# One saturating addition per half for the last sum and clip of q, and GpSimd's first product of a step behind the seeds of stage 0

## The chip, the cores and the metric

One core of one Trainium2 chip runs the whole program. The metric is the device time of that core in microseconds (us). TensorE (PE) multiplies matrices, and each of its matmuls has a weight load of its own (PEld) that overlaps the matmul before it. VectorE (DVE), ScalarE (ACT) and GpSimd (POOL) work on tiles of 128 partitions, each through its own queue in order, and the engines wait for each other by semaphores.

## The reference

The reference is a GRU over 32 steps, an attention over its states, and then a part on which this case turns: an oscillator integrated by Runge-Kutta over the same 32 steps, whose state q goes through a quantised feed-forward block at every step.

```
def _derivative(q, p, drive, coupling, bias):
    i_couple = jnp.tanh(q) @ coupling.T
    dq = q - q ** 3 / 3.0 - p + drive + i_couple + bias
    dp = EPSILON * (q + ALPHA - BETA * p)
    return (dq, dp)

def _rk4_step(q, p, drive, coupling, bias):
    dq1, dp1 = _derivative(q, p, ...)
    dq2, dp2 = _derivative(q + 0.5 * DT * dq1, p + 0.5 * DT * dp1, ...)
    dq3, dp3 = _derivative(q + 0.5 * DT * dq2, p + 0.5 * DT * dp2, ...)
    dq4, dp4 = _derivative(q + DT * dq3, p + DT * dp3, ...)
    q_next = q + DT / 6.0 * (dq1 + 2 * dq2 + 2 * dq3 + dq4)
    p_next = p + DT / 6.0 * (dp1 + 2 * dp2 + 2 * dp3 + dp4)
    q_next = jnp.clip(q_next, -CLAMP, CLAMP)
    p_next = jnp.clip(p_next, -CLAMP, CLAMP)
    return (q_next, p_next)
# per step, on q:  act_quant(q) -> silu(q @ w_gate) * (q @ w_up) -> act_quant -> @ w_down
```

q and p are 128 x 256 (256 features, batch 128), in float32; the feed-forward block has 832 middle features.

## The kernel before, in words

The GRU fills the span up to about 210 us, the attention goes to about 290 us, and the oscillator with the feed-forward block takes the rest: 32 steps of about 9.1 us. All engines follow an order written out by hand in the Python loops over t.

Features lie on partitions. q, p and all that belongs to them is held as 128 x 256: two halves m of 128 features, side by side. A step has four stages of the integration, called stage 0 to 3 here (slot 4t to 4t+3 in the code). A stage runs like this:

- DVE writes the seed (what does not go through the coupling matrix) of each half into PSUM: `seed_1` to `seed_4`, lines 1042, 1046, 1052 and 1060.
- ACT takes tanh of each half (L756) and the scaled square of both (L759). The stage's source is q itself in stage 0 and the result of the stage before in the others.
- PE adds the coupling product to the seed (`coupled`, L461), half by half, and counts s_ps for each. For half 0 it waits for the seed of half 0 and the first tanh, and then for the second tanh.
- DVE makes the cubic term (`cubic`, L1066, tile w_) from the square, and then the result of the stage (`nexts`, L1072): (PSUM times a factor) minus w_, once per half, counting s_next.

In stage 3 `nexts` puts its result into a spare part of PSUM, and a `tensor_scalar` with min and max (L1161) clips it to the new q, once per half. The new q starts the tanh of the next step, the seeds of stage 0 wait for s_next, PE transposes it (L486), and GpSimd adds it into t1.

GpSimd keeps the part that concerns p. In the order of a step: v1 (L1273, a product of p), then after both seeds of stage 0 uz and u3 (L1276, L1277, two more products of p), t1 = v1 + q (L1282), then W3 (L1290), an addition for the output (L1295), WZ (L1299), dq (L1301) and the new p (L1304). DVE carries t1 on to t2 (L1110), t3 (L1149) and t4 (L1154), from which GpSimd makes the new p.

The feed-forward block of earlier steps is woven into the same queues, one piece behind each stage. What bears on this case: on PE the seven transposes L497 behind stage 0 wait for hf, a 128 x 832 ACT operation (L775) that follows the square of stage 0; the block's second matmul pair L560 stands behind stage 3, ahead of the transposes of q; on DVE the `product` of sg and that matmul (L1085) stands right behind the seeds of stage 0, followed by the cubic term (L1066), a maximum over q (L1102), both `nexts` of stage 0 and the first seed of stage 1 (L1046). `product` waits for L560 (s_up) and for an earlier hf (s_hf).

Steps 0 to 2 differ: the feed-forward pieces come in one after another, and DVE prepares the weights in them (L983, L987).

## Time and profile before

| | us |
|---|---|
| median of 3 runs | 604.24 (603.88 to 604.67) |
| profiled execution, its own time | 603.75 |
| span of that execution | 601.70 |
| PE busy | 572.9 (95%) |
| DVE busy | 513.5 (85%) |
| ACT busy | 390.1 (65%) |
| POOL busy | 254.0 (42%) |

The profiled execution took 2.05 us beyond its span, which is what lies around the program's instructions. TensorE's mean granted clock is 0.997 of full speed. Busy time of PE includes matmuls that overlap, so 95% does not say that no other engine holds it up.

### The profile page before, as it was taken

To read this page: it belongs to the slowest core of one execution; us is meant where nothing else is said; L and a number is where in the kernel's file an instruction comes from. 1 tells how busy PE (TensorE), PEld (TensorE's weight loads), DVE (VectorE), ACT (ScalarE), POOL (GpSimd) and SP (SyncE) were. 2 spreads that over 40 slices of the span, in tenths; PEclk is the share of its full clock that TensorE was granted. 3 is DMA by queue.
4 is the path that set the end of the run, shared out by engine and by line. 5 is a ranking of instruction groups with operands and counts; after the bars stand their busy time and mean duration, and the time that the engine had idled before them with its cause. 6 is when DMAs were issued, how large, how long until landed. Compare 5 with 4: busy or idle time off the path is not lost.

```text
span 601.7 us, 15742 instructions
## 1 busy us (share of the span) xinstructions
PE 572.9 (95%) x5692; PEld 521.0 (87%) x5692; DVE 513.5 (85%) x1547; ACT 390.1 (65%) x959; POOL 254.0 (42%) x401
## 2 busy tenths in 40 slices
PE   9999999999999988999978999999999999999997
PEld 8999999999999887888867788888888888888885
DVE  3777767776777768998999999999999999999996
ACT  3554454444544453464556888898898888888885
POOL 0423323233232264240155556556555555555550
PEclk9999999999999998999999999999999999999999
DMA  8500000000000000500000000000000000000001
GB/s 259 187 2 2 1 1 2 1 1 2 1 1 1 19 3 2 190 4 3 1 1 1 11 19 16 15 19 10 18 20 10 19 20 10 19 19 11 17 19 37
DMA packets 12523, 14.97 MB, mean 25 GB/s; under 512 B 1632, under 2 KB 10144, under 8 KB 12448
## 3 DMA queue, kind: packets, MB, share of 16 engines
q1 hardware_dynamic: 12448, 13.97, 7.0%
q8 instruction: 47, 0.77, 0.5%
q14 instruction: 28, 0.23, 0.1%
HBM read 9.78 MB, written 4.19 MB: 23 GB/s over the span
## 4 chain that ended last, share of the span: by engine, by line
PE 73%; DVE 13%; ACT 11%; issue 3%; DVEq 0%; POOL 0%; ACTq 0%; POOLq 0%
PE PS L461 23%; PE PS L313 17%; PE PS L336 13%; ACT q_s L775 5%; PE PS L436 4%; PE PS L513 4%; PE PS L534 3%; PE PS L497 3%; ACT k_s L756 2%; DVE big L955 2%; PE PS L396 2%; PE PS L319 2%; DVE PS L1072 1%; ACT PS L759 1%; DVE h_s L1161 1%
## 5 line engine op out<-in xcount | busy, mean ns | idle before, releaser
L461 PE MATMUL PS<-k_s,h_s 128*128 128x128 f32 x1024 | 160.6, 284 | 4.2 <-DVE PS L1046 2.0
L461 PEld LDWEIGHTS PS<-k_s,h_s 128*128 128x128 f32 x1024 | 131.7, 191 | 21.1 <-DVE PS L1060 9.8
L313 PE MATMUL PS<-part 128*128 128x256 f32 x900 | 115.6, 286 | 0.0
L313 PEld LDWEIGHTS PS<-part 128*128 128x128 f32 x900 | 109.8, 191 | 0.0
L756 ACT ACTIVATE k_s<-h_s 128x128 f32<-128x128 f32 x256 | 69.1, 306 | 49.8 <-DVE h_s L1161 29.0
L336 PE MATMUL PS<-big,wrk 128*128 128x128 f32 x744 | 88.4, 275 | 1.7 <-DVE big L913 1.7
L336 PEld LDWEIGHTS PS<-big,wrk 128*128 128x128 f32 x744 | 85.8, 192 | 2.3 <-DVE big L913 2.3
L1229 POOL COPY h_s<-big 128x256 f32<-128x256 f32 x32 | 21.5, 671 | 128.9 <-DVE big L913 128.9
L461 PE MATMUL PS<-h_s 128*128 128x128 f32 x384 | 74.3, 275 | 0.0
L461 PEld LDWEIGHTS PS<-h_s 128*128 128x128 f32 x384 | 58.3, 192 | 0.0
L650 ACT ACTIVATE big<-big 128x256 f32<-128x256 f32 x32 | 13.3, 416 | 63.2 <-DVE big L895 63.2
L1066 DVE SCALAR_TENSOR_TENSOR h_s<-PS,h_s 128x256 f32<-128x256 f32 x128 | 52.7, 412 | 0.3 <-ACT PS L759 0.2
L1072 DVE SCALAR_TENSOR_TENSOR h_s<-PS,h_s 128x128 f32<-128x128 f32 x192 | 50.1, 285 | 2.2 <-PE PS L461 0.8
L759 ACT ACTIVATE PS<-h_s 128x256 f32<-128x256 f32 x128 | 47.2, 369 | 1.4 <-DVE part L961 1.4
L640 ACT ACTIVATE big<-PS,bg 128x256 f32<-128x256 f32 x96 | 41.2, 467 | 6.8 <-DVE bg L852 5.8
L1085 DVE SCALAR_TENSOR_TENSOR q_s<-PS,q_s 128x416 f32<-128x416 f32 x64 | 41.0, 644 | 0.8 <-PE PS L560 0.8
L652 ACT ACTIVATE big<-big 128x256 f32<-128x256 f32 x32 | 13.4, 418 | 38.9 <-DVE big L903 38.9
L1304 POOL TENSOR_SCALAR h_s<-q_s 128x256 f32<-128x256 f32 x31 | 12.5, 402 | 59.0 <-DVE q_s L1154 59.0
L1290 POOL TENSOR_TENSOR h_s<-h_s,k_s 128x256 f32<-128x256 f32 x32 | 25.0, 780 | 29.1 <-DVE q_s L1110 27.9
L899 DVE SCALAR_TENSOR_TENSOR big<-PS,bh,big 128x128 f32<-128x128 f32 x64 | 19.5, 346 | 18.0 <-ACT big L650 18.0
L1299 POOL TENSOR_TENSOR q_s<-h_s,k_s 128x256 f32<-128x256 f32 x32 | 23.9, 748 | 23.2 <-DVE PS L1052 23.2
L775 ACT ACTIVATE q_s<-q_s,mag 128x832 f32<-128x832 f32 x29 | 30.9, 1067 | 0.0
(189 smaller groups left out, 1244.9 us busy)
## 6 DMA issues: line engine op xcount, KB each, us to landing
out<-q_s SPq DMA_DIRECT2D x32, 128.0 KB, 1.7
x_s<-in_xT SPq DMA_DIRECT2D x14, 256.0 KB, 6.1
k_s<-in_wgT SPq DMA_DIRECT2D x1, 832.0 KB, 5.3
k_s<-in_wuT SPq DMA_DIRECT2D x1, 832.0 KB, 7.2
k_s<-in_wih SPq DMA_DIRECT2D x3, 256.0 KB, 4.1
wrk<-in_whh SPq DMA_DIRECT2D x3, 256.0 KB, 4.3
h_s<-in_wdT SPq DMA_DIRECT2D x1, 768.0 KB, 7.5
x_s<-in_xT SPq DMA_DIRECT2D x4, 128.0 KB, 3.6
```

Of the source, the lines that this page charges most:

```text
L313: r = pe.matmul(p, y, x, start=i == 0, stop=i == len(passes) - 1)
L336: r = pe.matmul(PS[:, bank, m * 128:(m + 1) * 128], whh_s[:, k, (m0 + m) * 128:(m0 + m + 1) * 128], hprev[:, k, :], start=k == 0, stop=k == 1)
L436: r = pe.matmul(PS[:, bank, :], raw(w), raw(x), start=k == 0 and n == 0, stop=k == 1 and n == 2)
L461: return pe.matmul(PS[:, m, 0:128], w, x, start=False, stop=True, skip_group_check=True)
L640: ac.activation(gi[:, n % 2, m, :], bulk_bank(u), ACT.Identity, bias=bg[:, m:m + 1]).then_inc(s_gi, 1)
L756: ac.activation(cm(th[slot % 2], m), cm(src, m), ACT.Tanh).then_inc(s_th, 1)
L759: ac.activation(sqP, src, ACT.Square, scale=math.sqrt(cube[s])).then_inc(s_sq, 1)
L775: ac.activation(hf[:, 0:NI], hN[i % 2], ACT.Identity, scale=h_at(i, 4), bias=mag[:, 0:1]).then_inc(s_hf, 1)
L1066: ve.scalar_tensor_tensor(w_, sqP, cube[s] * own[s], src, ALU.subtract, ALU.mult).then_inc(s_w, 1)
L1072: ve.scalar_tensor_tensor(dst(m), PS[:, m, 0:128], of_ps[slot % 4], cm(w_, m), ALU.mult, ALU.subtract).then_inc(s_next, 1)
L1085: ve.scalar_tensor_tensor(hN[i % 2][:, at], pg[:, g], q_at(i, 3), sg[:, at], ALU.mult, ALU.mult).then_inc(s_hN, 1)
L1290: po_.tensor_tensor(two(W3), two(u3), I_at(t), ALU.add).then_inc(s_W3, 1)
```

## The change

All of q's integration is now held multiplied by lam = 3/c4, with c4 = c/U as before. With that factor the last sum of stage 3 is PSUM + w_ with no factor on PSUM, and a custom DVE instruction, TENSOR_ADD_SAT, computes max(min(in0 + in1, s0), s1), which is sum and clip in one. It reads PSUM and w_, writes the new q in SBUF, and counts s_q. `nexts` of stage 3 and the two clips of L1161 are gone: four DVE instructions per step become two. Scale factors elsewhere (tanh, square, seeds, quantisation, the two start values) take up lam; they are immediates, and the copy of the start value becomes a `tensor_scalar`. The seeds of stage 0 change from `tensor_tensor` to `scalar_tensor_tensor` and wait for s_q. s_next counts six per step now (function q_next).

On GpSimd v1 waits for both seeds of stage 0 as well, and t1 comes right behind it, ahead of uz and u3.

```
+    lam = 3 / c4
+    of_ps = (3.0, 3.0, -6.0)
+    q_next = lambda t, s, m: 6 * t + 2 * s + m + 1
...
-                    ac.activation(cm(th[slot % 2], m), cm(src, m), ACT.Tanh).then_inc(s_th, 1)
+                        ac.wait_ge(s_next, q_next(slot // 4, s - 1, m))
+                    ac.activation(cm(th[slot % 2], m), cm(src, m), ACT.Tanh,
+                                  scale=(-1 if s == 3 else 1) / lam).then_inc(s_th, 1)
...
                 for m in range(2):
                     if t:
-                        ve.wait_ge(s_next, 8 * t - 1 + m)
-                    ve.tensor_tensor(PS[:, m, 0:128], I_at(t)[:, m], cm(pn[t % 2], m), ALU.subtract).then_inc(s_seed, 1)
+                        ve.wait_ge(s_q, 2 * t - 1 + m)
+                    ve.scalar_tensor_tensor(PS[:, m, 0:128], cm(pn[t % 2], m), -1 / lam, I_at(t)[:, m], ALU.mult,
+                                            ALU.add).then_inc(s_seed, 1)
...
+            def last_next(t):
+                ve.wait_ge(s_w, 4 * t + 4)
+                for m in range(2):
+                    ve.wait_ge(s_ps, 8 * t + 7 + m)
+                    ve._custom_dve(bass.dve_ops.TENSOR_ADD_SAT, out=cm(qn[(t + 1) % 2], m), in0=PS[:, m, 0:128],
+                                   in1=cm(w_, m), s0=CLAMP * lam, s1=-CLAMP * lam).then_inc(s_q, 1)
...
-                nexts(4 * t + 3, lambda m: PS[:, m, 128:256])
-                for m in range(2):
-                    ve.wait_ge(s_next, 8 * t + 7 + m)
-                    ve.tensor_scalar(cm(qn[(t + 1) % 2], m), PS[:, m, 128:256], CLAMP, -CLAMP, ALU.min,
-                                     ALU.max).then_inc(s_q, 1)
+                last_next(t)
...
+                if t:
+                    po_.wait_ge(s_seed, 8 * t + 2)
                 if t < T - 1:
                     po_.tensor_scalar(v1, p, horner[0], 0.0, ALU.mult, ALU.add).then_inc(s_v1, 1)
-                if t:
-                    po_.wait_ge(s_seed, 8 * t + 2)
-                po_.tensor_scalar(uz, p, -n3, 0.0, ALU.mult, ALU.add).then_inc(s_uz, 1)
-                po_.tensor_scalar(u3, p, -n2, 0.0, ALU.mult, ALU.add).then_inc(s_u3, 1)
-                if t < T - 1:
-                    if t:
-                        po_.wait_ge(s_q, 2 * t)
                     po_.wait_ge(s_v1, t + 1)
                     po_.tensor_tensor(t1, v1, q, ALU.add).then_inc(s_t1, 1)
+                po_.tensor_scalar(uz, p, -n3 / lam, 0.0, ALU.mult, ALU.add).then_inc(s_uz, 1)
+                po_.tensor_scalar(u3, p, -n2 / lam, 0.0, ALU.mult, ALU.add).then_inc(s_u3, 1)
```

DVE's queue before, from t4 of a step past the boundary to the first seed of the next step's stage 1; h_s and q_s are the memory in which q, the stages' results and the products lie:

```order
L1154 SCALAR_TENSOR_TENSOR q_s<-q_s,h_s 128x256
L1157 RECIPROCAL q_s<-q_s 128x1
L1072 SCALAR_TENSOR_TENSOR PS<-PS,h_s 128x128 x2
L1161 TENSOR_SCALAR h_s<-PS 128x128 x2
L1042 TENSOR_TENSOR PS<-k_s,h_s 128x128 x2
L1085 SCALAR_TENSOR_TENSOR q_s<-PS,q_s 128x416
L1066 SCALAR_TENSOR_TENSOR h_s<-PS,h_s 128x256
L1102 TENSOR_REDUCE q_s<-PS 128x1
L1072 SCALAR_TENSOR_TENSOR h_s<-PS,h_s 128x128 x2
L1046 SCALAR_TENSOR_TENSOR PS<-h_s,k_s 128x128
```

The same place now, with the new line numbers (1083 the saturating addition, 1045 the seeds of stage 0, 1096 the product, 1050 the seed of stage 1):

```order
L1165 SCALAR_TENSOR_TENSOR q_s<-q_s,h_s 128x256
L1168 RECIPROCAL q_s<-q_s 128x1
L1083 ISA h_s<-PS,h_s 128x128 x2
L1045 SCALAR_TENSOR_TENSOR PS<-h_s,k_s 128x128 x2
L1096 SCALAR_TENSOR_TENSOR q_s<-PS,q_s 128x416
L1070 SCALAR_TENSOR_TENSOR h_s<-PS,h_s 128x256
L1113 TENSOR_REDUCE q_s<-PS 128x1
L1076 SCALAR_TENSOR_TENSOR h_s<-PS,h_s 128x128 x2
L1050 SCALAR_TENSOR_TENSOR PS<-h_s,k_s 128x128
```

Only the two L1161 have left this queue; the two L1072 ahead of them have become the two L1083, and nothing else stands in another place.

GpSimd's queue before, from the new p (L1304) to W3 (L1290):

```order
L1304 TENSOR_SCALAR h_s<-q_s 128x256
L1273 TENSOR_SCALAR h_s<-h_s 128x256
L1276 TENSOR_SCALAR h_s<-h_s 128x256
L1277 TENSOR_SCALAR h_s<-h_s 128x256
L1282 TENSOR_TENSOR q_s<-h_s 128x256
L1290 TENSOR_TENSOR h_s<-h_s,k_s 128x256
```

and now (1308 the new p, 1282 v1, 1284 t1, 1285 and 1286 uz and u3, 1294 W3):

```order
L1308 TENSOR_SCALAR h_s<-q_s 128x256
L1282 TENSOR_SCALAR h_s<-h_s 128x256
L1284 TENSOR_TENSOR q_s<-h_s 128x256
L1285 TENSOR_SCALAR h_s<-h_s 128x256
L1286 TENSOR_SCALAR h_s<-h_s 128x256
L1294 TENSOR_TENSOR h_s<-h_s,k_s 128x256
```

t1, the `tensor_tensor`, has moved ahead of uz and u3, which now stand last of the four before W3.

## Rows read from the trace of the kernel before

**Rows 1.** The page's chain that ended last, shares of the span.

```profile
PE 73%; DVE 13%; ACT 11%; issue 3%; DVEq 0%; POOL 0%; ACTq 0%; POOLq 0%
```

**Rows 2.** Chain over one boundary of steps: start us, us, what.

```profile
452.08 0.20 DVE h_s L1161
...
452.31 0.51 ACT k_s L756 x2
...
453.09 1.01 ACT q_s L775
```

**Rows 3.** Timeline, same boundary: start us, us, engine, line, tiles [idle before <-releaser].

```profile
451.34 0.28 DVE L1072 SCALAR_TENSOR_TENSOR PS<-PS,h_s 128x128 f32<-128x128 f32 x1
451.44 0.40 POOL L1304 TENSOR_SCALAR h_s<-q_s 128x256 f32<-128x256 f32 x1 [1.92 <-DVE q_s L1154]
451.79 0.30 DVE L1072 SCALAR_TENSOR_TENSOR PS<-PS,h_s 128x128 f32<-128x128 f32 x1 [0.16 <-PE PS L461]
451.80 0.87 PE L560 MATMUL PS<-h_s,q_s 128*128 128x416 bf16 x4
451.93 0.41 POOL L1273 TENSOR_SCALAR h_s<-h_s 128x256 f32<-128x256 f32 x1
451.99 0.48 DVE L1161 TENSOR_SCALAR h_s<-PS 128x128 f32<-128x128 f32 x2
452.39 0.49 DVE L1042 TENSOR_TENSOR PS<-k_s,h_s 128x128 f32<-128x128 f32 x2
452.76 1.13 PE L461 MATMUL PS<-k_s,h_s 128*128 128x128 f32 x8
452.79 0.65 DVE L1085 SCALAR_TENSOR_TENSOR q_s<-PS,q_s 128x416 f32<-128x416 f32 x1
452.96 0.41 POOL L1276 TENSOR_SCALAR h_s<-h_s 128x256 f32<-128x256 f32 x1 [0.63 <-DVE PS L1042]
453.33 0.41 POOL L1277 TENSOR_SCALAR h_s<-h_s 128x256 f32<-128x256 f32 x1
453.70 0.73 POOL L1282 TENSOR_TENSOR q_s<-h_s 128x256 f32<-128x256 f32 x1
454.24 0.55 PE L497 MATMUL PS<-identh,q_s 128*128 128x128 f16 x7 [0.35 <-ACT q_s L775]
454.41 0.29 DVE L1046 SCALAR_TENSOR_TENSOR PS<-h_s,k_s 128x128 f32<-128x128 f32 x1
454.75 0.52 PEld L461 LDWEIGHTS PS<-k_s,h_s 128*128 128x128 f32 x4
```

**Rows 4.** DVE alone in a GRU step, timeline.

```profile
105.37 0.61 DVE L899 SCALAR_TENSOR_TENSOR big<-PS,bh,big 128x128 f32<-128x128 f32 x2 [0.55 <-ACT big L650]
106.01 0.42 DVE L903 TENSOR_TENSOR big<-big 128x256 f32<-128x256 f32 x1
...
107.60 0.42 DVE L909 TENSOR_TENSOR big<-big 128x256 f32<-128x256 f32 x1
108.12 0.43 DVE L913 TENSOR_TENSOR big<-big 128x256 f32<-128x256 f32 x1
```

**Rows 5.** The page's group of L899: count | busy us, mean ns | idle before.

```profile
L899 DVE SCALAR_TENSOR_TENSOR big<-PS,bh,big 128x128 f32<-128x128 f32 x64 | 19.5, 346 | 18.0 <-ACT big L650 18.0
```

**Rows 6.** Step 1, stage 0 and the start of stage 1, timeline.

```profile
307.17 0.72 POOL L1282 TENSOR_TENSOR q_s<-h_s 128x256 f32<-128x256 f32 x1
307.55 0.50 DVE L1046 SCALAR_TENSOR_TENSOR PS<-h_s,k_s 128x128 f32<-128x128 f32 x1
308.10 0.71 PE L461 MATMUL PS<-k_s,h_s 128*128 128x128 f32 x4 [1.05 <-DVE PS L1046]
```

**Rows 7.** Timeline, the product in step 2.

```profile
316.70 0.65 DVE L1085 SCALAR_TENSOR_TENSOR q_s<-PS,q_s 128x416 f32<-128x416 f32 x1 [0.80 <-PE PS L560]
```

**Rows 8.** Chain at the end of the last step.

```profile
588.32 0.70 PE PS L560 x4
589.02 0.23 PE PS L581 x2
```

More of the change, by code:

```diff
@@ L754, in stage @@
                     else:
-                        ac.wait_ge(s_next, 2 * slot - 1 + m)
-                    ac.activation(cm(th[slot % 2], m), cm(src, m), ACT.Tanh).then_inc(s_th, 1)
+                        ac.wait_ge(s_next, q_next(slot // 4, s - 1, m))
+                    ac.activation(cm(th[slot % 2], m), cm(src, m), ACT.Tanh,
+                                  scale=(-1 if s == 3 else 1) / lam).then_inc(s_th, 1)
                 if slot == 0:
                     ac.wait_ge(s_F, 16)
-                ac.activation(sqP, src, ACT.Square, scale=math.sqrt(cube[s])).then_inc(s_sq, 1)
+                ac.activation(sqP, src, ACT.Square, scale=math.sqrt(cube[s]) / lam).then_inc(s_sq, 1)
             for t in range(T):
@@ L992, in start_values @@
                 ve.wait_ge(s_S, 8)
-                ve.tensor_copy(qn[0], condf)
-                ve.tensor_scalar(pn[0], condf, SH, U, ALU.subtract, ALU.mult).then_inc(s_q0, 1)
+                ve.tensor_scalar(qn[0], condf, lam, None, ALU.mult)
+                ve.tensor_scalar(pn[0], condf, SH, U * lam, ALU.subtract, ALU.mult).then_inc(s_q0, 1)
                 ve.wait_ge(ld_cb, 16)
@@ L1050, in seed_3 @@
                 ve.wait_ge(s_W3, t + 1)
-                ve.wait_ge(s_next, 8 * t + 3 + m)
-                ve.scalar_tensor_tensor(PS[:, m, 0:128], cm(qn[t % 2], m), (1 + 2 * A * kap) / (2 * c4), cm(W3, m),
+                ve.wait_ge(s_next, q_next(t, 1, m))
+                ve.scalar_tensor_tensor(PS[:, m, 0:128], cm(qn[t % 2], m), (1 + 2 * A * kap) / 6, cm(W3, m),
                                         ALU.mult, ALU.add).then_inc(s_seed, 1)
@@ L1058, in seed_4 @@
                 for m in range(2):
-                    ve.wait_ge(s_next, 8 * t + 5 + m)
-                    ve.scalar_tensor_tensor(PS[:, m, 0:128], cm(dq, m), 1 / c4, cm(WZ, m), ALU.mult,
+                    ve.wait_ge(s_next, q_next(t, 2, m))
+                    ve.scalar_tensor_tensor(PS[:, m, 0:128], cm(dq, m), 1 / 3, cm(WZ, m), ALU.mult,
                                             ALU.add).then_inc(s_seed, 1)
@@ L1108, in vector @@
                     ve.wait_ge(s_t1, t + 1)
-                    ve.wait_ge(s_next, 8 * t + 2)
+                    ve.wait_ge(s_next, q_next(t, 0, 1))
                     ve.scalar_tensor_tensor(t2, t1, horner[1], qs[0], ALU.mult, ALU.add).then_inc(s_t2, 1)
@@ L1114, in vector @@
                         ve.wait_ge(s_wvec, 3)
-                    ve.scalar_tensor_tensor(q_at(i, 1, 3), wide(q_at(i, 0), 3), TINY, wvec[:, 0:3], ALU.max,
+                    ve.scalar_tensor_tensor(q_at(i, 1, 3), wide(q_at(i, 0), 3), TINY * lam, wvec[:, 0:3], ALU.max,
                                             ALU.mult).then_inc(s_tq, 1)
@@ L1147, in vector @@
                     ve.wait_ge(s_t2, t + 1)
-                    ve.wait_ge(s_next, 8 * t + 4)
+                    ve.wait_ge(s_next, q_next(t, 1, 1))
                     ve.scalar_tensor_tensor(t3, t2, horner[2], qs[1], ALU.mult, ALU.add).then_inc(s_t3, 1)
@@ L1152, in vector @@
                     ve.wait_ge(s_t3, t + 1)
-                    ve.wait_ge(s_next, 8 * t + 6)
-                    ve.scalar_tensor_tensor(t4, t3, horner[3], qs[2], ALU.mult, ALU.add).then_inc(s_t4, 1)
+                    ve.wait_ge(s_next, q_next(t, 2, 1))
+                    ve.scalar_tensor_tensor(t4, t3, horner[3], qs[2], ALU.mult, ALU.subtract).then_inc(s_t4, 1)
                 if t >= 2:
@@ L1181, in vector @@
             ve.wait_ge(s_red, T)
-            ve.scalar_tensor_tensor(q_at(i, 1, 3), wide(q_at(i, 0), 3), TINY, wvec[:, 0:3], ALU.max,
+            ve.scalar_tensor_tensor(q_at(i, 1, 3), wide(q_at(i, 0), 3), TINY * lam, wvec[:, 0:3], ALU.max,
                                     ALU.mult).then_inc(s_tq, 1)
@@ L1260, in gpsimd @@
                     po_.tensor_scalar(coupU, coup, U, 0.0, ALU.mult, ALU.add).then_inc(s_cp, 1)
-                    for dst, f in ((id_q1, (1 - kap) / c4), (id_s2, -kap / c4), (id_z3, (2 - 2 * kap) / c4)):
+                    for dst, f in ((id_q1, (1 - kap) / 3), (id_s2, -kap / 3), (id_z3, (2 - 2 * kap) / 3)):
                         po_.tensor_scalar(dst, ident[:, :], f, 0.0, ALU.mult, ALU.add).then_inc(s_cp, 1)
@@ L1299, in gpsimd @@
                 po_.tensor_tensor(two(WZ), two(uz), I_at(t), ALU.add).then_inc(s_WZ, 1)
-                po_.wait_ge(s_next, 8 * t + 2)
+                po_.wait_ge(s_next, q_next(t, 0, 1))
                 po_.tensor_tensor(dq, qs[0], q, ALU.subtract).then_inc(s_dq, 1)
@@ L1303, in gpsimd @@
                     po_.wait_ge(s_t4, t + 1)
-                    po_.tensor_scalar(pn[(t + 1) % 2], t4, (CLAMP - SH) * U, (-CLAMP - SH) * U, ALU.min,
+                    po_.tensor_scalar(pn[(t + 1) % 2], t4, (CLAMP - SH) * U * lam, (-CLAMP - SH) * U * lam, ALU.min,
                                       ALU.max).then_inc(s_p, 1)
```

9 lines of the change are left out of this document (4 added, 5 removed).

## The prediction

> **What bounds the kernel now.** I read the chain of waits first, then the timeline of one boundary between steps, engine by engine, because the chain names only one of the paths that meet there. The chain gives PE 73%, DVE 13% and ACT 11% of the span [rows 1]. Across a boundary it goes from the second clip (0.20 us of its own), to the two tanh, the square and the 1.01 us of L775 on ACT, and then to PE's transposes L497 [rows 2], which begin after 0.35 us of idle time [rows 3]. Read alone, this says that the clip is on the path in each step.
>
> The timeline shows a second path that is as tight. Behind the seeds of stage 0, DVE starts the product L1085 at 452.79, and from there it has no gap until L1046, the first seed of stage 1, starts at 454.41: 1.62 us of product, cubic term, maximum and two sums, back to back. L1046 ends at 454.70, and PE's weight load for stage 1 starts at 454.75 [rows 3]. That load cannot come sooner, however early L497 is done. And the product waits not only for the seeds: it reads the result of L560, whose last matmul ends at 451.80 + 0.87 = 452.67 [rows 3]. L560 is PE's work, behind stage 3, and nothing in it depends on the clip.
>
> How long after that release can the product start? From step 4 on it has two waits (s_up and s_hf). A DVE instruction with one wait starts 0.03 us after its releaser ends (L899 to L903: 105.98, 106.01); one with two starts 0.10 us after it (L909 to L913: 108.02, 108.12) [rows 4]. So the earliest start is 452.77, against 452.79 now. Up to 0.02 us of slack is all that DVE has there.
>
> **The change part by part.** *The clips, 64 instructions, and the sums, 64 that become saturating additions.* The second sum is released by PE and starts at 451.79, before and after. What follows moves up by 0.40 us on DVE: the seeds of stage 0 from 452.39 to 451.99, ending at 452.48 in place of 452.88. The second tanh starts 0.04 us after the addition ends, at 452.12 in place of 452.31 + 0.20 = 452.51, so tanh, square and L775 move by 0.39 us, and L497 could start at 453.85, before PE is done with stage 0 (452.76 + 1.13 = 453.89) [rows 2, 3]. The 0.35 us of idle time of PE goes. What is late next is the first seed of stage 1: it moves only by the product's 0.00 to 0.02 us, and PE waits for it after L497 in place of before. PE's own order ahead of the boundary is unchanged, so the gain is 0.00 to 0.02 us in each of the 29 boundaries from that into step 3 to that into step 31. I take the middle, 0.01: 29 x 0.01 = 0.3 us, with ends of 0 and 0.6.
>
> *The price of the new instruction.* No row has it. The nearest is the instruction it replaces, the same shape and operands: 0.28 to 0.30 us [rows 3]. The longest row of a 128x128 operation of DVE with a PSUM and an SBUF operand is L899, 0.346 us on average [rows 5], so I bound it at 0.28 and 0.35. A longer one would be hidden towards DVE's product and ACT by the 0.4 us just won; not towards GpSimd (below). I take 0.29, no difference. The Trainium skill (Vector Engine (DVE) Microarchitecture Reference, "Rate slope and fixed cost") says that measured programs of several micro-operations pay the same fixed cost as built-in ones; no run shown here has one, and it would give the same sum.
>
> *The seeds of stage 0* become a form that L1046 has already: 0.29 us each for one and the other [rows 3]. The scale factors are immediates of instructions that run anyway. One start-value copy changes its form, once: nothing.
>
> *GpSimd: v1 behind the seeds, t1 first.* Before, v1 ran at 451.93 to 452.34, which is just where the seeds would now stand; it would have met them. Now four instructions start behind the seeds. Seeds end at 452.48; GpSimd starts 0.08 us after its releaser (452.88, 452.96); a product takes 0.41, a dependent one starts 0.09 after the end of its source (L1304 ends at 451.84, L1273 starts at 451.93), t1 takes 0.73, and an independent one starts 0.04 before the end of the one ahead [rows 3]. That gives v1 452.56 to 452.97, t1 453.06 to 453.79, uz 453.75 to 454.16, u3 454.12 to 454.53. DVE takes t1 right behind L1046 (from 454.6), so t1 gains room; W3 waits for t2, which comes after that too, so u3 is in time. But u3 still runs when L1046 wants to start, at 454.39 to 454.41, with 0.12 to 0.14 us to go.
>
> Does that hurt? L1046 reads p and the drive, both in SBUF. In step 1 it started in the middle of t1 on GpSimd (307.17 to 307.89) and took 0.50 us in place of 0.29: it ended at 308.05, 0.16 us behind t1 [rows 6]. So it can bear a GpSimd operation that ends up to 0.29 - 0.16 = 0.13 us after its own start at no cost. u3 ends 0.12 to 0.14 after it. The cost is 0 to 0.01 us a step by these rows; I take 0. The Trainium skill (SBUF — State Buffer, "Who interferes with whom") states the rule behind this: a DVE instruction with two SBUF inputs contends with a GpSimd instruction that reads SBUF. It also says that the one that comes second "fully blocks" until the first is finished; what that would make of the time stands under the second rival.
>
> *Step 1.* There L1085 does not exist yet, and PE waits 1.05 us for L1046 [rows 6], so DVE's 0.40 us come through. The 0.21 us for which t1 held up L1046 go as well, since t1 is then nearly done, but uz and u3 now stand where t2 and the second seed want to read. I take 0.3 us of gain, with ends of 0 and 0.6. At the boundary into step 2 the product waits 0.80 us for L560 with DVE idle [rows 7]: nothing to gain. At the very end PE takes the transposes L581 right behind L560 (588.32 + 0.70 = 589.02) [rows 8]; q is there before that, so nothing either.
>
> *Sum.* 0.3 + 0.3 = 0.6 us off the profiled execution's 603.75: 603.15. The median of the runs is 604.24, 0.49 above that execution, so I forecast 604.24 - 0.6 = **603.6 us**, with 602.9 to 604.8 as this case's own range.
>
> **The rivals.** *First, the chain is right and the boundary shortens.* Then each step gains PE's idle 0.35 us before L497 [rows 3]: 29 x 0.35 = 10.2 us, 594. For it: the page's chain, and PE's large share. Against it: DVE's 1.62 us without a gap, and a product that cannot start before L560. It would take a product that gets free earlier, or a seed of stage 1 that PE does not wait for. Chance 0.12, part of the gain included.
>
> *Second, slower: the seed of stage 1 falls behind u3 on GpSimd.* The place is L1046 against u3, in the 28 steps 3 to 30. The margin is 0.13 us against 0.12 to 0.14. It decides as soon as u3 ends later than 0.13 us after the seed's start: each 0.01 us beyond that costs 28 x 0.01 = 0.28 us. A saturating addition of 0.35 us brings 0.05 to 0.06, and 28 x 0.06 = 1.7, less the 0.6 gained: 605.3. If the seed is held until u3 ends and then runs its full 0.29 us, it ends at 454.53 + 0.29 = 454.82 in place of 454.70, 28 x 0.12 = 3.4 us, less the 0.3 of step 1: 607.3. That second form is the skill's "fully blocks" read literally; the row of 0.50 us speaks against it, since full blocking would have made 0.34 + 0.29 = 0.63 [rows 6]. For the rival: the margin is thinner than what I can read. Chance 0.28.
>
> *Third, the saved DVE time is hidden and step 1 gains nothing:* 604.2, inside the forecast's own range, and not counted apart. The chance of the forecast is 0.60.
>
> **How the numbers follow.** A measurement of this kernel can tell about 0.2% from no change, 1.2 us here: 603.0 to 605.4. Of the forecast's 0.60, 0.05 falls below that. Faster: 0.12 + 0.05 = 0.17. The slower rival gives 0.25 above the limit and 0.03 below it. Same: 0.55 + 0.03 = 0.58. Slower: 0.25. The range reaches down to 602.2, which leaves out most of the first rival, and up to 607.3, the second rival's full blocking.
>
> **What would show it.** In the profile after, L497 should have no idle time behind L775, and PE's load of stage 1 should wait about 0.3 us for the seed L1050 instead; DVE should stand idle for some 0.3 us before the product L1096, released by L560. If DVE has no idle time there, the product is not bound by L560 as I say. L1050 should take 0.29 us; 0.30 or more, with u3 (L1286) ending over 0.13 us after its start, is the second rival. The saturating addition should take 0.28 to 0.30 us. The step should last 9.06 to 9.08 us; 8.7 is the first rival. The time outside of the span should stay near 2.05 us.

## The result, and the profile after

| | before | after |
|---|---|---|
| median of 20 runs each, us | 603.86 | 605.54 |
| lowest to highest | 601.86 to 604.67 | 603.47 to 606.17 |
| profiled execution, its span | 603.75, 601.70 | 605.59, 603.6 |
| median step of the oscillator (steps 3 to 30) | 9.077 | 9.125 |

The ratio of after to before is 1.0024, with a 95% interval of 1.0013 to 1.0034: slower by some 1.4 us (the two medians differ by 1.7). A step here lasts from the first seed of stage 0 to the first seed of stage 0 of the next step; its length is taken from the timeline. What lies around the span is 605.59 - 603.6 = 2.0 us, as before. Executions of every kernel, the one before included, come in two groups some 1.7 us apart (the last section shows what tells them apart), so small differences are compared within a group below.

The chain after gives ACT 3% in place of 11% and DVE 18% in place of 13%; it now lies where the prediction had put the second path:

```profile
PE 74%; DVE 18%; issue 4%; ACT 3%; DVEq 0%; POOL 0%; ACTq 0%; POOLq 0%
```

The chain of waits over the boundary that answers to [rows 2] (start us, us, what):

```profile
452.48 0.72 PE PS L562 x4
...
453.30 0.61 DVE q_s L1096
...
454.20 0.41 DVE q_s L1113
454.61 0.40 DVE h_s L1076 x2
455.01 0.26 DVE PS L1050
...
455.31 1.60 PE PS L463 x12
```

It goes from PE's matmul pair (L560 before, L562 now) through the product, the maximum, the two sums and the seed of stage 1 back to PE. The tanh, the square and the long ACT operation are off it.

The timeline of the boundary, which answers to [rows 3]:

```profile
452.30 0.29 DVE L1083 CUSTOM_DVE_ANT_0 h_s<-PS,h_s 128x128 f32<-128x128 f32 x1 [0.17 <-PE PS L463]
452.31 0.87 PE L562 MATMUL PS<-h_s,q_s 128*128 128x416 bf16 x4
452.51 0.49 DVE L1045 SCALAR_TENSOR_TENSOR PS<-h_s,k_s 128x128 f32<-128x128 f32 x2
453.15 0.41 POOL L1282 TENSOR_SCALAR h_s<-h_s 128x256 f32<-128x256 f32 x1 [0.79 <-DVE PS L1045]
453.30 0.65 DVE L1096 SCALAR_TENSOR_TENSOR q_s<-PS,q_s 128x416 f32<-128x416 f32 x1 [0.30 <-PE PS L562]
...
454.36 0.55 PE L499 MATMUL PS<-identh,q_s 128*128 128x128 f16 x7
454.71 0.41 POOL L1286 TENSOR_SCALAR h_s<-h_s 128x256 f32<-128x256 f32 x1
454.93 0.33 DVE L1050 SCALAR_TENSOR_TENSOR PS<-h_s,k_s 128x128 f32<-128x128 f32 x1
455.31 0.52 PEld L463 LDWEIGHTS PS<-k_s,h_s 128*128 128x128 f32 x4 [0.58 <-DVE PS L1050]
455.31 0.71 PE L463 MATMUL PS<-k_s,h_s 128*128 128x128 f32 x4 [0.41 <-DVE PS L1050]
```

Three things are to be seen. The transposes (L499) have no idle time in front of them any more, and PE waits 0.41 us after them for the seed L1050: the wait has changed its place. DVE stands idle for 0.30 us before the product, which starts 0.12 us after the matmul pair ends (452.31 + 0.87 = 453.18). And the seed starts at 454.93 while u3 on GpSimd (L1286) runs to 454.71 + 0.41 = 455.12; it takes 0.33 us in place of the 0.29 of [rows 3].

The two instructions over the whole run (durations in ns: shortest, median, longest):

```profile
L1050 DVE SCALAR_TENSOR_TENSOR PS<-h_s,k_s x64: 285/291/416, 298.5 to 583.9; 128x128 f32<-128x128 f32 x64
L1083 DVE CUSTOM_DVE_ANT_0 h_s<-PS,h_s x64: 270/291/293, 304.9 to 590.1; 128x128 f32<-128x128 f32 x64
```

The saturating addition costs what the sum before it cost. L1050's 64 are two kinds: the second seeds of a step have a median of 286 ns, the first ones, which meet u3, 337 ns.

Step 1, which answers to [rows 6]:

```profile
307.02 0.72 POOL L1284 TENSOR_TENSOR q_s<-h_s 128x256 f32<-128x256 f32 x1
307.64 0.29 DVE L1050 SCALAR_TENSOR_TENSOR PS<-h_s,k_s 128x128 f32<-128x128 f32 x1
...
308.02 0.68 PE L463 MATMUL PS<-k_s,h_s 128*128 128x128 f32 x4 [0.83 <-DVE PS L1050]
```

The seed takes its 0.29 us here, not 0.50; t1 ends only 0.10 us after the seed's start. Step 1 lasts 9.187 us in place of 9.866.

**The account.** The ordinary step is 0.048 us longer: 28 x 0.048 = 1.34. Single steps are longer than the ordinary one by 0.129 (step 20), 0.292 (23), 0.095 (25), 0.163 (26) and 0.258 (29), together 0.94, where before only step 22 was, by 0.161: 0.78 more. Step 1 gives back 0.68. Step 0 is 0.39 shorter, and from the first seed of step 31 to the end it takes 0.37 longer, which is the seeds' moving ahead alone. Together 1.34 + 0.78 - 0.68 - 0.39 + 0.37 = 1.4 us, which is the measured difference. (The two profiled spans differ by 1.9 us; the other 0.5 us lie ahead of the first seed.) The first part is the collision with u3; the second, over half as large, was in none of my cases.

A usual step, and step 23 at the same place, both of the kernel after, DVE alone:

```profile
457.16 0.49 DVE L1056 SCALAR_TENSOR_TENSOR PS<-h_s 128x128 f32<-128x128 f32 x2
```

```profile
512.05 0.29 DVE L1056 SCALAR_TENSOR_TENSOR PS<-h_s 128x128 f32<-128x128 f32 x1
512.59 0.30 DVE L1056 SCALAR_TENSOR_TENSOR PS<-h_s 128x128 f32<-128x128 f32 x1 [0.25 <-issue]
```

The two seeds of stage 2 follow each other without a gap in a usual step; in step 23 the second comes 0.34 us late, and its idle time has no releaser but "issue". It is the 1600th instruction recorded on DVE, where a second wait is a record of its own and counts. The others are the 1472nd (step 20), the 1729th (26) and the 1856th (29): each 64 or 65 above a multiple of 128. The one late instruction before was the 1601st. On GpSimd the 453rd is late, in step 25 (v1: idle for 1.08 us before it in place of 0.79).

### The profile page after: what moved, and what is told of

Its sections match the earlier page's. It is cut to its first block, busy times and chain, and to the rows that moved or that the text cites. A ratio compares the mean times of both kernels' runs of the same rounds, so it can differ in the third digit from the quotient of the medians.

```text
span 603.6 us, 15678 instructions
## 1 busy us (share of the span) xinstructions
PE 571.7 (95%) x5692; PEld 521.2 (86%) x5692; DVE 504.7 (84%) x1483; ACT 393.1 (65%) x959; POOL 254.8 (42%) x401
## 4 chain that ended last, share of the span: by engine, by line
PE 74%; DVE 18%; issue 4%; ACT 3%; DVEq 0%; POOL 0%; ACTq 0%; POOLq 0%
PE PS L463 22%; PE PS L315 18%; PE PS L338 13%; PE PS L562 4%; PE PS L438 4%; PE PS L515 3%; PE PS L536 3%; DVE q_s L1096 3%; DVE h_s L1076 3%; DVE big L958 2%; PE PS L398 2%; DVE q_s L1113 2%; PE PS L321 2%; DVE PS L1050 1%; PE PS L553 1%
## 5 line engine op out<-in xcount | busy, mean ns | idle before, releaser
L758 ACT ACTIVATE k_s<-h_s 128x128 f32<-128x128 f32 x256 | 71.9, 307 | 48.2 <-DVE h_s L1076 30.4
```

The costliest lines, as they stand in the source:

```text
L758: ac.activation(cm(th[slot % 2], m), cm(src, m), ACT.Tanh, scale=(-1 if s == 3 else 1) / lam).then_inc(s_th, 1)
```

## The experiments

Times are medians in us, ratios are to the kernel before beside which each kernel ran. "Full clock" is the difference to the kernel before among executions with a granted clock of 1.000 (0.999 in two) alone, "0.997" among the others; the ratio mixes both groups. A group can be small: one run for e3 at 0.997 and for e17 at full clock, two for e4 at full clock. "By steps" is the change that the steps of the one profiled execution add up to, from the first seed to the end, against the profiled execution of before.

| kernel | median (before) | ratio | step | by steps | full clock | 0.997 |
|---|---|---|---|---|---|---|
| after | 605.54 (603.86) | 1.0024 [1.0013, 1.0034] | 9.125 | +1.4 | | |
| e1 without u3 | 602.95 (603.41) | 0.9999 [0.9986, 1.0011] | 9.079 | +0.3 | 0.0 | +0.5 |
| e2 additions, old order | 603.22 (603.41) | 0.9997 [0.9985, 1.0009] | 9.079 | +0.4 | +0.2 | +0.2 |
| e3 clips, new order | 612.77 (603.41) | 1.0156 [1.0139, 1.0173] | 9.417 | +9.9 | +9.7 | +10.1 |
| e4 matmul pair first | 601.94 (603.41) | 0.9963 [0.9950, 0.9977] | 9.000 | -2.1 | -2.7 | -2.5 |
| e6 the same on before | 603.46 (602.57) | 1.0005 [0.9991, 1.0019] | 9.076 | 0.0 | 0.0 | +0.1 |
| e10 25 instructions ahead | 604.34 (602.57) | 1.0023 [1.0011, 1.0035] | 9.125 | +1.1 | +1.0 | +0.9 |
| e12 GpSimd spread | 603.11 (602.57) | 1.0006 [0.9993, 1.0018] | 9.083 | +0.3 | +0.4 | +0.1 |
| e13 spread, pair first | 597.06 (602.57) | 0.9905 [0.9889, 0.9922] | 8.863 | -5.9 | -6.1 | -6.2 |
| e16 one wait | 603.09 (602.71) | 1.0001 [0.9988, 1.0013] | 9.079 | 0.0 | -0.1 | +0.1 |
| e18 one wait, 28 ahead | 603.47 (602.71) | 0.9996 [0.9983, 1.0008] | 9.079 | -0.5 | -0.6 | -0.4 |
| e17 e13, one wait, 28 ahead | 596.90 (602.71) | 0.9894 [0.9876, 0.9911] | 8.863 | -6.8 | -7.2 | -6.7 |

The sum over the steps agrees with the timed difference within 0.6 us in each row, so an account by steps can be trusted to about that much.

### Is it u3? (e1, e2, e3)

e1 takes u3 away and makes W3 from uz, so its results of stage 2 are not those of the reference:

```
-                po_.tensor_scalar(u3, p, -n2 / lam, 0.0, ALU.mult, ALU.add).then_inc(s_u3, 1)
...
-                po_.wait_ge(s_u3, t + 1)
-                po_.tensor_tensor(two(W3), two(u3), I_at(t), ALU.add).then_inc(s_W3, 1)
+                po_.wait_ge(s_uz, t + 1)
+                po_.tensor_tensor(two(W3), two(uz), I_at(t), ALU.add).then_inc(s_W3, 1)
```

> The changed kernel with GpSimd's product u3 left out (W3 is made from uz, so the results of stage 2 differ from the reference). Theory (the first seed of stage 1, L1050, is held up by the read of u3 on GpSimd, which ends 0.19 us after the seed's start, and a step is 9.125 us long for it in place of 9.077): uz is now the last of the products and ends about 0.17 us before the seed starts, the seed takes 0.29 us in place of 0.33 and the step falls back to 9.07 to 9.08 us; about 604.2 where the changed kernel is 605.5, so 0.998 to 1.001 times the kernel before. Rival (the saturating addition itself or the wait for the second matmul pair costs the 0.05 us per step): the step stays at 9.12 us and the ratio at 1.002.

Its timeline at the seed of stage 1:

```profile
454.12 0.41 POOL L1285 TENSOR_SCALAR h_s<-h_s 128x256 f32<-128x256 f32 x1
...
454.71 0.29 DVE L1050 SCALAR_TENSOR_TENSOR PS<-h_s,k_s 128x128 f32<-128x128 f32 x1
```

GpSimd is done at 454.53 and the seed takes 0.29 us. The step falls from 9.125 to 9.079: the 0.048 us a step are u3's. The long steps 20, 23, 26 and 29 stay, with 0.126, 0.313, 0.163 and 0.259 us, so they are not u3's. Step 25 is ordinary in this run, whose GpSimd queue is shorter.

e2 keeps the saturating additions and puts GpSimd's instructions back in the order of before:

```
+                if t < T - 1:
+                    po_.tensor_scalar(v1, p, horner[0], 0.0, ALU.mult, ALU.add).then_inc(s_v1, 1)
                 if t:
                     po_.wait_ge(s_seed, 8 * t + 2)
+                po_.tensor_scalar(uz, p, -n3 / lam, 0.0, ALU.mult, ALU.add).then_inc(s_uz, 1)
+                po_.tensor_scalar(u3, p, -n2 / lam, 0.0, ALU.mult, ALU.add).then_inc(s_u3, 1)
                 if t < T - 1:
-                    po_.tensor_scalar(v1, p, horner[0], 0.0, ALU.mult, ALU.add).then_inc(s_v1, 1)
+                    if t:
+                        po_.wait_ge(s_q, 2 * t)
                     po_.wait_ge(s_v1, t + 1)
                     po_.tensor_tensor(t1, v1, q, ALU.add).then_inc(s_t1, 1)
-                po_.tensor_scalar(uz, p, -n3 / lam, 0.0, ALU.mult, ALU.add).then_inc(s_uz, 1)
-                po_.tensor_scalar(u3, p, -n2 / lam, 0.0, ALU.mult, ALU.add).then_inc(s_u3, 1)
```

> The changed kernel with GpSimd's order of the kernel before (v1 as soon as p is there, then behind the seeds of stage 0 uz, u3, t1). Theory: v1 now runs at the time at which the seeds of stage 0 want to read, so the first of them takes about 0.5 us in place of 0.29; nobody waits for that, since DVE has 0.3 us of idle time before the product and PE starts stage 0 only later. t1 ends before or with the start of the first seed of stage 1, so that seed takes 0.29 us and the step is 9.07 to 9.08 us. With what the early steps gained (about 1 us in the profile) 603.0 to 603.8, ratio 0.998 to 1.000. Rival (the collision of v1 with the seeds is what has to be kept away): the step gets longer than 9.125 us, ratio above 1.0024.

```profile
450.89 0.41 POOL L1280 TENSOR_SCALAR h_s<-h_s 128x256 f32<-128x256 f32 x1
450.95 0.69 DVE L1045 SCALAR_TENSOR_TENSOR PS<-h_s,k_s 128x128 f32<-128x128 f32 x2
...
451.75 0.65 DVE L1096 SCALAR_TENSOR_TENSOR q_s<-PS,q_s 128x416 f32<-128x416 f32 x1
```

v1 (L1280 here) now meets the seeds of stage 0: the first of them takes 0.484 us in place of 0.290 (median). It costs nothing, since DVE has 0.30 us to spare before the product: the seeds end at 451.64, the product starts at 451.75. The step is 9.079 again. So the second half of the change, moving v1 behind the seeds, avoided a collision that was free and made one that was not.

e3 does the opposite, the clips of before with GpSimd's new order:

```
-                if t < T - 1:
-                    po_.tensor_scalar(v1, p, horner[0], 0.0, ALU.mult, ALU.add).then_inc(s_v1, 1)
                 if t:
                     po_.wait_ge(s_seed, 8 * t + 2)
-                po_.tensor_scalar(uz, p, -n3, 0.0, ALU.mult, ALU.add).then_inc(s_uz, 1)
-                po_.tensor_scalar(u3, p, -n2, 0.0, ALU.mult, ALU.add).then_inc(s_u3, 1)
                 if t < T - 1:
+                    po_.tensor_scalar(v1, p, horner[0], 0.0, ALU.mult, ALU.add).then_inc(s_v1, 1)
                     if t:
...
+                po_.tensor_scalar(uz, p, -n3, 0.0, ALU.mult, ALU.add).then_inc(s_uz, 1)
+                po_.tensor_scalar(u3, p, -n2, 0.0, ALU.mult, ALU.add).then_inc(s_u3, 1)
```

> The kernel before (sum and clip apart) with GpSimd's new order alone. Theory (a seed that finds GpSimd reading ends about 0.15 us after GpSimd's operation): the seeds of stage 0 end 0.4 us later than in the changed kernel, so u3 ends 0.4 us later too, some 0.57 us after the start of the first seed of stage 1. That seed ends 0.43 us late, PE waits for it, and the step is 9.077 + 0.43 = 9.5 us in the 28 steps from 3 to 30: 12 us more, 616, ratio 1.018 to 1.021. Rival (GpSimd's order costs nothing and the saturating addition is what made the changed kernel slower): the step stays at 9.08 us, ratio 0.999 to 1.001.

```profile
458.48 0.55 POOL L1280 TENSOR_SCALAR h_s<-h_s 128x256 f32<-128x256 f32 x1
458.48 0.29 DVE L1046 SCALAR_TENSOR_TENSOR PS<-h_s,k_s 128x128 f32<-128x128 f32 x1
458.68 0.62 DVE L1110 SCALAR_TENSOR_TENSOR q_s<-q_s,h_s 128x256 f32<-128x256 f32 x1
...
459.00 0.57 POOL L1281 TENSOR_SCALAR h_s<-h_s 128x256 f32<-128x256 f32 x1
459.22 0.35 DVE L1115 SCALAR_TENSOR_TENSOR q_s<-q_s 128x3 f32<-128x3 f32 x1
...
459.49 0.29 DVE L1046 SCALAR_TENSOR_TENSOR PS<-h_s,k_s 128x128 f32<-128x128 f32 x1
...
459.83 0.52 PEld L461 LDWEIGHTS PS<-k_s,h_s 128*128 128x128 f32 x4 [0.26 <-DVE PS L1046]
```

The step grew by 0.34 us, not by the 0.43 that I had expected, and by another way. I had thought the first seed would be held by uz. It came first and uz (L1280) was held instead, 0.55 us in place of 0.41. But then t2 (L1110) was held by uz, 0.62 in place of 0.42, the three columns of L1115 by u3, 0.35 in place of 0.16, and so the second seed came late, for which PE's load waited 0.26. A collision that is not on the seed that PE waits for first can be dearer than one that is.

### How many waits (e16)

In after, v1 waits for the new p (s_p) and for both seeds (s_seed). The seeds wait for the new q, which needs the whole step, so the second wait covers the first, and v1 is behind the new p in GpSimd's own queue. e16 drops it:

```
                 if t:
-                    po_.wait_ge(s_p, t)
+                    po_.wait_ge(s_seed, 8 * t + 2)
                 else:
                     po_.wait_ge(s_q0, 1)
-                if t:
-                    po_.wait_ge(s_seed, 8 * t + 2)
```

> The changed kernel with one wait fewer ahead of v1 on GpSimd: the wait for the new p goes, since the seeds of stage 0, for which v1 waits too, have waited for it. Theory (v1 starts 0.16 us after the seeds with two waits and 0.08 us with one; so u3 ends 0.19 us after the start of the first seed of stage 1, beyond the 0.13 us that the seed can bear): v1 starts 0.08 us after the seeds, u3 ends 0.12 us after the seed's start, the seed takes 0.29 us and the step is 9.075 to 9.085 us; the long steps 20, 23, 26, 29 stay; ratio 0.999 to 1.001. Rival (the held seed has another cause than u3's end, or the second wait costs nothing): 9.125 us a step, ratio 1.0024.

```profile
450.08 0.49 DVE L1045 SCALAR_TENSOR_TENSOR PS<-h_s,k_s 128x128 f32<-128x128 f32 x2
...
450.65 0.40 POOL L1280 TENSOR_SCALAR h_s<-h_s 128x256 f32<-128x256 f32 x1 [0.72 <-DVE PS L1045]
...
452.21 0.41 POOL L1284 TENSOR_SCALAR h_s<-h_s 128x256 f32<-128x256 f32 x1
...
452.50 0.29 DVE L1050 SCALAR_TENSOR_TENSOR PS<-h_s,k_s 128x128 f32<-128x128 f32 x1
```

v1 starts 450.65 - (450.08 + 0.49) = 0.08 us after the seeds; in the kernel after it was 453.15 - (452.51 + 0.49) = 0.15. u3 ends 452.62 - 452.50 = 0.12 us after the seed's start, as the prediction had it, and the seed takes 0.288 us (median). The step is 9.079. So all but 0.002 of the 0.048 us a step comes from one wait too many ahead of v1. DVE's long steps stay (0.122, 0.291, 0.159, 0.257); step 25 is ordinary here too, where GpSimd's queue has one record fewer a step.

### Where the late instructions stand (e10, e18)

e10 puts 25 one-column memsets of a new, unused tile into DVE's queue at the start of the program; nothing else changes:

```
+        spare = sb("spare", [128, 32])
...
             ve.memset(mag[:, :], MAGIC).then_inc(s_mag, 1)
+            for j in range(25):
+                ve.memset(spare[:, j:j + 1], 0.0)
```

> The changed kernel with 25 tiny memsets (128x1, into an unused tile) at the start of DVE's queue, while DVE waits for its first loads. In the traces so far single steps are 0.1 to 0.3 us longer than the rest (steps 20, 23, 26 and 29 in the changed kernel, only step 22 in the one before), and the late DVE instruction is each time one whose number in DVE's queue is 64 more than a multiple of 128. Theory (something in DVE's queue comes late every 128 instructions; the changed kernel has 43 a step, so it falls on the seeds of stage 2 over and over, and the kernel before has 45, so it wanders): 25 more instructions ahead move it to where DVE waits for PE anyway, and the long steps go: 0.8 us less than the changed kernel, with 0.3 us less behind the last step; ratio to the kernel before 1.0005 in place of 1.0024, steps of 9.12 to 9.13 us as before. Rival (the long steps hang on the saturating addition or on chance): they stay at steps 20, 23, 26, 29, ratio 1.0024.

If the late instructions belonged to their step or their tile, they would stay. They moved: steps 20, 23, 26 and 29 are ordinary now, and steps 8 (+0.302) and 14 (+0.096) are long, where DVE's 960th and 1216th instruction stand, again 64 above a multiple of 128; steps 16 and 17 add 0.09 together. Step 25 keeps its 0.095, which is GpSimd's. Step 8, at the 960th:

```profile
369.93 0.65 DVE L1099 SCALAR_TENSOR_TENSOR q_s<-PS,q_s 128x416 f32<-128x416 f32 x1 [0.65 <-PE PS L563]
```

It is the product, 0.65 us idle in place of 0.30. The place was as I had thought, the gain was not: I had expected a ratio of 1.0005 and measured 1.0023. Only 0.34 us went, since the same number falls on other places that also count.

The traces show what else happens at these places. The page of the kernel after lists 28 transfers of instructions on one DMA queue, of 8192 bytes each (queue, kind: transfers, MB, share of 16 engines):

```profile
q14 instruction: 28, 0.23, 0.1%
```

8192 bytes are 64 for each of 128 instructions. One of these transfers starts 0.71, 0.79, 0.61 and 0.73 us after the start of the late instruction in steps 20, 23, 26 and 29, and 0.65 us after that of GpSimd's in step 25. It is so with those that cost nothing as well: over the 13 traces, 168 of the 208 DVE instructions whose number is 64 above a multiple of 128 have such a transfer starting within 1 us behind them, against 21 of 1419 at seven other places of the 128 (0, 16, 32, 48, 80, 96 and 112 above). So an instruction comes late where DVE's instructions are fetched. It doesn't wait for that transfer to arrive, since it runs before the transfer starts.

That a queue of 45 a step is not safe by itself shows in e3, which has 45: its steps 5, 14 and 22 are longer by 0.29, 0.29 and 0.24 us, 0.81 in all. Late there are GpSimd's 197th and 325th instruction, 128 apart, and DVE's 1601st, each with a transfer 0.6 to 0.8 us behind its start.

e18 is e16 with 28 memsets at the same place:

```
             ve.memset(mag[:, :], MAGIC).then_inc(s_mag, 1)
+            for j in range(28):
+                ve.memset(spare[:, j:j + 1], 0.0)
```

> The same with 28 tiny memsets at the start of DVE's queue. Theory (both losses of the changed kernel lifted: the held seed, 1.3 us, and the late instruction every 128, 0.8 us): steps of 9.08 us, at most 0.3 us in all of longer single steps between step 3 and step 30, and what step 1 gained stays; 0.5 to 0.8 us less than the kernel before, ratio 0.998 to 1.0. Rival (the place of the late instruction has nothing to do with the count): steps 20, 23, 26 and 29 are long again, 0.8 us in all, ratio 1.0 to 1.001.

Of the long steps of e16, 0.83 us together, 0.32 are left (steps 5 and 7). Against the kernel before it is 0.6 us faster at full clock and 0.4 at 0.997; e16 was level with it. The 0.5 us between them are the late instructions' share that this shift hides. The ratio over all runs, 0.9996, doesn't tell it from no change; the sum over the steps (-0.5) and both groups of runs do agree on it. This is close to what the change would have brought with neither loss. That it comes out near the 0.6 us of the prediction is luck: none of it is won at the ordinary boundaries, which were to give 0.3.

### What the freed time on DVE is worth (e4, e6, e12, e13, e17)

After the change DVE waits for the matmul pair, which stands behind other transposes. e4 puts the pair ahead of them:

```
+                if t >= 1:
+                    i = t - 1
...
+                            r = pe.matmul(pg[:, g], qiT[:, k, :], wu_q[:, k, g * 416:(g + 1) * 416],
+                                          start=k == 0, stop=k == 1)
+                    r.then_inc(s_up, 1)
                 if t >= 2:
...
                     r.then_inc(s_x1t, 1)
-                if t >= 1:
-                    i = t - 1
...
-                            r = pe.matmul(pg[:, g], qiT[:, k, :], wu_q[:, k, g * 416:(g + 1) * 416],
-                                          start=k == 0, stop=k == 1)
-                    r.then_inc(s_up, 1)
```

> The changed kernel with PE's second matmul pair of the feed-forward block ahead of the two transposes of x, so that the product's release comes 0.22 us sooner. Theory (two holds in a row: the product waits for that matmul pair, and the first seed of stage 1 waits for u3 on GpSimd): the product starts 0.2 us sooner, but the seed still ends 0.14 us behind u3 and takes 0.5 us or more; the step stays at 9.11 to 9.13 us, ratio 1.001 to 1.003. Rival (GpSimd does not hold the seed, the matmul pair alone sets the step): 8.90 us a step, 6 us less, ratio 0.992 to 0.994.

```profile
452.45 0.29 DVE L1050 SCALAR_TENSOR_TENSOR PS<-h_s,k_s 128x128 f32<-128x128 f32 x1
452.45 0.54 POOL L1286 TENSOR_SCALAR h_s<-h_s 128x256 f32<-128x256 f32 x1
452.65 0.62 DVE L1121 SCALAR_TENSOR_TENSOR q_s<-q_s,h_s 128x256 f32<-128x256 f32 x1
...
453.26 0.29 DVE L1050 SCALAR_TENSOR_TENSOR PS<-h_s,k_s 128x128 f32<-128x128 f32 x1
```

I had expected 9.11 to 9.13 us a step, all of the gain eaten by u3; it was 9.000. The seed came in just ahead of u3, which was held instead (0.54 us); the price went to t2 (L1121, 0.62 in place of 0.42) and to the second seed. The kernel is 0.37% faster than before.

e6 makes the same edit to the kernel before.

> The kernel before, with only PE's second matmul pair ahead of the two transposes of x. Theory (in the kernel before the clip keeps DVE busy up to the product, so the pair's earlier end is worth nothing without the saturating addition): the step stays at 9.07 to 9.08 us, ratio 0.999 to 1.001. Rival (the pair's place alone brings what the combination brings): 9.00 us a step or less, ratio 0.996.

Nothing, as expected: there the product's other releaser, the end of DVE's own clips and seeds, is as late as the pair. Neither edit gives much alone; the two paths are tied, and each edit shortens one.

e12 is after with GpSimd's work spread over the step: only v1, t1 and u3 right behind the seeds of stage 0, uz after W3, and the output addition behind the seeds of stage 3.

```
-                po_.tensor_scalar(uz, p, -n3 / lam, 0.0, ALU.mult, ALU.add).then_inc(s_uz, 1)
                 po_.tensor_scalar(u3, p, -n2 / lam, 0.0, ALU.mult, ALU.add).then_inc(s_u3, 1)
...
                 po_.tensor_tensor(two(W3), two(u3), I_at(t), ALU.add).then_inc(s_W3, 1)
-                if t >= 4:
-                    i = t - 4
-                    po_.wait_ge(s_x1k, i + 1)
-                    po_.wait_ge(s_osc, i + 1)
-                    po_.tensor_tensor(ob[i % 2], ob[i % 2], x1n[i % 2], ALU.add).then_inc(s_out, 1)
+                po_.tensor_scalar(uz, p, -n3 / lam, 0.0, ALU.mult, ALU.add).then_inc(s_uz, 1)
...
                 po_.tensor_tensor(dq, qs[0], q, ALU.subtract).then_inc(s_dq, 1)
+                if t >= 4:
+                    i = t - 4
+                    po_.wait_ge(s_seed, 8 * t + 8)
+                    po_.wait_ge(s_x1k, i + 1)
+                    po_.wait_ge(s_osc, i + 1)
+                    po_.tensor_tensor(ob[i % 2], ob[i % 2], x1n[i % 2], ALU.add).then_inc(s_out, 1)
```

> The changed kernel with GpSimd's work spread otherwise: behind the seeds of stage 0 v1, t1 and u3 only, uz between W3 and the seeds of stage 2, and the addition for the output behind the seeds of stage 3, where GpSimd waited 1.9 us before. Theory (the first seed of stage 1 was held by u3; with that gone the product's wait for PE's second matmul pair is what sets the step): u3 ends 0.2 us before the seed starts, the seed takes 0.29 us, a step 9.07 to 9.08 us, as in the run without u3; ratio 0.999 to 1.001. Rival (GpSimd's products merely collide elsewhere): 9.12 us or more.

Alone it takes off the collision (seed 0.293 us, step 9.083) and no more. u3 ends 0.06 us ahead of the seed's start (452.27, 452.33), not the 0.2 us that I had expected. With the pair first as well, it is e13:

> The same with PE's second matmul pair ahead of the two transposes of x. Theory (two holds, both lifted now): the product starts at the end of the seeds of stage 0, 0.35 us sooner against the boundary, the second sum of stage 0 is then released by PE, and PE starts stage 1 about 0.25 us sooner: 8.80 to 8.87 us a step, 6 to 7.5 us less than the kernel before, ratio 0.988 to 0.991. Rival (some third hold was as tight as these two, so that moving the pair brings no more than the 0.08 us it brought to the changed kernel): 9.00 us a step, ratio 0.996.

```profile
448.95 0.50 DVE L1045 SCALAR_TENSOR_TENSOR PS<-h_s,k_s 128x128 f32<-128x128 f32 x2
...
449.43 0.65 DVE L1096 SCALAR_TENSOR_TENSOR q_s<-PS,q_s 128x416 f32<-128x416 f32 x1
...
450.80 0.41 POOL L1285 TENSOR_SCALAR h_s<-h_s 128x256 f32<-128x256 f32 x1
...
451.06 0.29 DVE L1050 SCALAR_TENSOR_TENSOR PS<-h_s,k_s 128x128 f32<-128x128 f32 x1
```

The product follows the seeds at once, the seed of stage 1 starts 2.11 us after the first seed of stage 0 (in the kernel after 454.93 - 452.51 = 2.42), and u3 (L1285 here) ends 0.15 us after its start at no cost. The step is 8.863 us, the kernel 0.95% faster than before (0.9889 to 0.9922). The page's chain now names DVE first:

```profile
DVE 45%; PE 43%; issue 8%; ACT 3%; DMA 1%; SPq 1%; DVEq 0%; ACTq 0%
```

e17 adds the single wait and the 28 memsets:

> The fastest so far (GpSimd's work spread, PE's matmul pair first), with both of these edits. Theory: the seed of stage 1 does not meet u3 there, so one wait fewer brings little by itself; the long steps of 0.8 us go. A step 8.83 to 8.87 us, ratio 0.988 to 0.990 where it was 0.9905. Rival (DVE sets the step there and the late instruction costs wherever it falls, since DVE has no idle time left): the long steps move but stay 0.8 us in all, ratio 0.990 to 0.991.

It has the same step of 8.863, and 0.8 us less in the single steps. At 596.90 us (0.9894, 0.9876 to 0.9911) it is the fastest kernel of this case; against e13 it gains 0.9 us at 0.997 (597.22, 4 runs, to 598.10, 3 runs) and 1.1 at full clock, where it has one run.

## Why the prediction was wrong

The forecast was 603.6 us and no change that can be told; what came was 605.54, a loss of 0.24%. That is outside of the forecast's own 602.9 to 604.8, and inside the wide range of 602.2 to 607.3, which took in the second rival. That rival, with 0.28, was the one that happened, at its place, though not for the reason it gave, and it is 1.34 of the 2.12 us that were lost. Two steps failed: the start of GpSimd's work behind the seeds, read 0.07 us too early, and the late instructions, a cost that the sum did not have.

- *The two tied paths.* Right. PE's 0.35 us before the transposes are gone and stand, as 0.41 us, before stage 1's matmuls. The first rival, which read the chain alone, would have made the step 8.7 us.
- *The product is bound by the matmul pair.* Right: 0.30 us idle, released by L562, in each of the 29 boundaries. The gain of 0.00 to 0.02 us in each was 0: e1 and e16, with no collision, have 9.079 us against 9.077. I had taken 0.01, which is 0.3 us.
- *The price of the saturating addition.* Right: 291 ns (median), of 0.28 to 0.30 us.
- *"GpSimd starts 0.08 us after its releaser".* Wrong, and the step on which the collision hung. That 0.08 us was read before an instruction with one wait [rows 3]. v1 has two, and starts 0.15 us after. I had read in [rows 4] that a second wait costs DVE 0.07 us, and had used it for the product, but not for GpSimd, 0.07 us being just what the margin could not bear. u3 thus ends 0.19 us after the seed's start, not 0.12 to 0.14, and the seed takes 0.048 us longer: 28 x 0.048 = 1.34 us. e16 gives all but 0.06 us of it back by dropping the wait.
- *The hold itself.* The bound of 0.13 us was near: 0.12 cost nothing in e16, 0.15 next to nothing in e13 (294 ns, median), 0.19 cost 0.045. The held seed ends 0.14 us after u3, which puts the bound at 0.29 - 0.14 = 0.15, a little above mine. The Trainium skill (SBUF — State Buffer, "Who interferes with whom") says that the one that comes second is fully blocked. It says so of DVE's 2-port modes; for an instruction with two SBUF inputs, as here, it has an exclusive lock. The runs agree with that only if the lock holds up the part that moves data. A DVE instruction of 128 columns takes 0.29 us here and one of 256 takes 0.42, so 128 columns are 0.13 us and the rest is fixed. The held instructions of 128 columns end 0.13 to 0.16 us after the GpSimd instruction (L1050 in after 0.14, L1045 in e2 0.13, L1046 in [rows 6] 0.16), those of 256 columns 0.27 and 0.28 (L1110 in e3, L1121 in e4). So the columns run after the lock is free, and the fixed part before. A third width fits: L1115 in e3 has 3 columns and ends with u3, at 459.57 both. That reading was worked out after the runs; no run varied the width on purpose.
- *Step 1.* The sign was right, the size was not: 0.68 us, where I had taken 0.3 with an end of 0.6. uz and u3 did not get in the way of the seed for which PE waits.
- *The late instructions.* Missed altogether, a term put at nothing: 0.78 us. The change takes DVE's queue from 45 to 43 instructions a step. Three steps of 43 are 129, so every 128th instruction falls within one place of where the last one fell, around the seeds of stage 2, and four times it fell where it counts. With 45 a step (three are 135) it wanders by 7, and in the kernel before all but one were hidden. The distance of 128, the shift by added instructions (e10, e18) and the transfer of instructions right behind each late one are shown. By what the fetch holds up the instruction is not. The Trainium skill (Runtime: NRT & Kernel Launch, "Instruction fetch mechanics") has the engine refill its instructions in blocks of 256 and calls the crossing mostly hidden. Here the block is 128 instructions on DVE, and a crossing on the path costs 0.1 to 0.35 us.
- *The sum.* Forecast -0.3 (boundaries) - 0.3 (step 1) = -0.6. Measured 0 - 0.68 + 1.34 + 0.78 = +1.4. Nearly without the two losses the change is worth the -0.5 us of e18. Two terms at the ends, which the sum did not have, cancel: step 0 is 0.39 us shorter and the stretch behind the last step 0.37 longer.
- *A reading of the chain.* The 0.20 us in [rows 2] belong to the first clip, which ends at 452.27 in the trace and releases the tanh at 452.31, not to the second. No term of the sum hangs on it.

What stays open: what in the fetch makes an instruction late, why some are late by 0.1 us and others by 0.35, and which of them the kernel before hides.

## What to carry to other kernels

Count the waits ahead of an instruction, not only the latest of them: a redundant one, already implied by another, cost 0.07 us at each start here, and where two engines pass each other by a tenth of a microsecond it decides. A margin as thin as the reading's own error is no result to forecast; the better edit is to move the neighbour away, as e12 did. Where two paths are tied, shortening one brought little or nothing here (e2, e6) and both together did (e13), and in a long unrolled loop a changed number of instructions per step is itself a change: look whether single steps are longer than the rest.
